# Routed experts of a two-layer mixture kernel: blocks 0 to 3 by sorted rows in place of dense tiles

## The chip, the cores and the metric

One NeuronCore of a Trainium2 chip runs the kernel. The metric is the device time of one execution in microseconds (us), the median of the runs. TensorE is called PE in the rows, its weight loads PEld, VectorE DVE, ScalarE ACT, GpSimd POOL, and SyncE SP; SPq is SP's queue of DMA issues.

## What is computed

The reference adds two layers to x of 32 x 128 tokens with 128 features. Each layer is a conditioning block followed by a feed-forward block. The change is within the conditioning block of the second layer (`_L1_cond_ref`), of which this is the part that matters:

```python
for e in range(N_SHARED):                       # 2 shared experts
    h = silu(x @ s_w1[e].T) * (x @ s_w3[e].T)
    shared_out = shared_out + h @ s_w2[e].T
s = sigmoid(router_in @ W_router.T)             # 8 experts
_, topk_idx = top_k(s + router_bias, 2)
s_sel = take_along_axis(s, topk_idx, axis=1)
gates = where(denom > 1e-09, s_sel / (denom + 1e-09), 1.0 / TOP_K)
for e in range(8):                              # 8 routed experts
    h = gelu(x @ r_w1[e].T)
    routed_out = routed_out + h @ r_w2[e].T * gates_full[:, e:e + 1]
out = (shared_out / 2 + routed_out) / 4
```

A token has a gate other than zero for 2 of the 8 routed experts. The feed-forward block behind it is of low rank: P = x U1, H = gelu(P V1 + b1), y = (H U2) V2 + b2, with rank 32, and the token's x is added.

## The kernel before

The 4096 tokens lie transposed (features on the 128 partitions) in NBLK = 8 blocks of BLK = 512 tokens. fp32 accuracy comes from fp32r matmuls on high and low parts: an up projection of a tile is three of them (high weights by high tokens, low by high, high by low), so is a down projection in the first layer; behind the second layer's hidden tiles the down weights are folded with U1 into WD, four copies of 32 columns, and a down projection is two matmuls, with the high part HH and the low part HL of the hidden tile.

`plan()` writes the work as one list of items. A and G are the conditioning of layer one, B its eight experts (8 experts x 8 blocks x 4 tiles, expert outermost). The second layer's items are S (shared, 4 a block, two up projections each), R (routed, 8 a block, one for each expert over all 512 tokens) and F (feed-forward, 4 a block). The order there is S0 S1 R0 R1, S2 S3 F0 F1 R2 R3, S4 S5 F2 F3 R4 R5, S6 S7 F4 R6 R7, F5 F6 F7, where S0 is all of block 0's S items.

An item has a slot k in the list. TensorE issues its up projection at slot k and its down projection LAG = 5 slots later (`up`, `down`). In between VectorE and ScalarE make the hidden tile Hf (for R: gelu in place, then VectorE multiplies by the gates, line 1558), ScalarE or VectorE its high part HH (lines 1084, 1568) and GpSimd or VectorE its low part HL (lines 1663, 1571), by the item's `hi_act` and `lo_pool`. PSUM has four banks for up projections, two for down sums, two for small uses. The program of each engine is written out in the order of k; engines keep to each other only by semaphores, so SP can run ahead of TensorE.

The routing runs in `choose(g, k)` on VectorE in ten steps for each half g of the blocks (0 to 3 and 4 to 7), at the slots `pick`. The gates are turned by TensorE, copied to q3, written to DRAM (line 730) and from there broadcast to 128 partitions by SP, 256 KB for each block and expert (line 658), into CWB, ST and TMP (`gate_place`). SP's queue also brings the weights of layer one's experts (ST<-in_wb_dram), the combine weights of layer one (CWB<-scratch, line 755), and the weights of layer two (ST<-in_wc_dram, line 737), which VectorE and GpSimd split at the slots `split_wc` (lines 1504, 1611). In G, tokens are brought by DMAs whose address comes from a register: a TENSOR_LOAD on SP brings the register's value (line 761), then the DMA is issued (line 771).

## Time and profile before

| | us |
|---|---|
| median of 3 runs | 889.8 (889.48 to 890.18) |
| span of the profiled execution | 886.9 |
| PE busy | 870.3 (98%) |
| DVE busy | 682.8 (77%) |
| ACT busy | 574.0 (65%) |
| POOL busy | 402.0 (45%) |
| SP's queue q1, share of 16 DMA engines | 30.1% |

The profile is of one execution. Its span runs from the first to the last instruction, and the runs' device time holds what lies around it. A matmul in the rows is shown with its latency, so a busy PE does not mean one at its peak: the distance of two starts is the pace. The layer-two part begins at 703.1 us and is some 184 us long.

### The profile page before, as it was taken

The page shows a single profiled execution, that of the slowest core. Times are in us where ns is not written, and L with a number is a line of the kernel's source. Part 1 is how long each engine was busy: PE and PEld are TensorE (multiplying, and loading weights), DVE is VectorE, ACT ScalarE, POOL GpSimd, SP SyncE. Part 2 cuts the span into 40 slices and gives each one's busy share as a digit, 9 for nine tenths or more (in the row PEclk, how much of TensorE's full clock was granted, in tenths as well). Part 3 has the DMA queues.
Part 4 walks back from the last instruction along what each step waited for, and adds up shares of the span by engine and source line. Part 5 has one row for each costly group of instructions (what it writes and reads, how often), then busy time and mean ns, then how long its engine had stood idle before and what let it go on. Part 6 is the DMA issues. An engine that isn't in the chain of part 4 may idle for free.

```text
span 886.9 us, 12606 instructions
## 1 busy us (share of the span) xinstructions
PE 870.3 (98%) x3838; PEld 690.2 (78%) x3838; DVE 682.8 (77%) x1094; ACT 574.0 (65%) x1029; POOL 402.0 (45%) x376
## 2 busy tenths in 40 slices
PE   8999999999999999999999999999999999999997
PEld 5788888777888888888888888888888777777773
DVE  7877777869689786686686686686665888998887
ACT  7888888765555455555555555555555678989895
POOL 7557783135356453253253252252232227754462
PEclk9999999999999999999999999999999999999999
DMA  9589981023113112012012012011010049582700
GB/s 311 211 276 313 293 295 35 1 86 135 48 48 111 42 42 84 4 45 84 1 48 83 1 48 84 0 48 48 1 48 0 1 108 209 106 178 53 161 25 36
DMA packets 36404, 83.23 MB, mean 94 GB/s; under 512 B 4464, under 2 KB 14320, under 8 KB 34544
## 3 DMA queue, kind: packets, MB, share of 16 engines
q1 hardware_dynamic: 36336, 82.42, 30.1%
q8 instruction: 31, 0.51, 0.2%
q14 instruction: 37, 0.30, 0.1%
HBM read 71.39 MB, written 6.83 MB: 88 GB/s over the span
## 4 chain that ended last, share of the span: by engine, by line
PE 76%; DVE 9%; issue 4%; ACT 3%; SPq 3%; DMA 2%; POOL 1%; DVEq 0%; ACTq 0%; POOLq 0%
PE ps L932 16%; PE ps L951 16%; PE ps L937 16%; PE ps L992 8%; PE ps L994 8%; PE ps L987 8%; DVE HL L1571 3%; SPq L658 1%; PE ps L974 1%; PE ps L972 1%; DVE Hf L1551 1%; DMA ST<-scratch 1%; DVE Hf L1558 1%; ACT HH L1084 1%; SPq L771 1%
## 5 line engine op out<-in xcount | busy, mean ns | idle before, releaser
L1078 ACT ACTIVATE Sg<-ps 128x512 f32<-128x512 f32 x288 | 171.7, 597 | 242.6 <-PE ps L951 242.3
L1551 DVE TENSOR_TENSOR Hf<-ps,Sg 128x512 f32<-128x512 f32 x288 | 197.9, 688 | 147.7 <-ACT Sg L1078 97.5
L1663 POOL TENSOR_TENSOR HL<-Hf,HH 128x512 fp32r<-128x512 f32 x130 | 174.2, 1347 | 157.4 <-ACT HH L1084 141.0
L1084 ACT ACTIVATE HH<-Hf 128x512 fp32r<-128x512 f32 x346 | 216.1, 625 | 21.1 <-DVE Hf L1551 14.4
L1571 DVE TENSOR_TENSOR HL<-Hf,HH 128x512 fp32r<-128x512 f32 x248 | 220.1, 888 | 4.3 <-ACT HH L1084 3.2
L932 PE MATMUL ps<-XHL,WBH 128*128 128x512 f32 x512 | 203.7, 398 | 1.8 <-DVE Hf L1551 1.8
L951 PE MATMUL ps<-XHL,WBH 128*128 128x512 f32 x512 | 202.2, 395 | 0.0
L937 PE MATMUL ps<-XHL,WBL 128*128 128x512 f32 x512 | 202.0, 395 | 0.0
L1678 POOL TENSOR_TENSOR XT<-XT,TMP 128x512 f32<-128x512 f32 x64 | 84.0, 1312 | 248.9 <-DVE TMP L1425 248.7
L932 PEld LDWEIGHTS ps<-XHL,WBH 128*128 128x128 f32 x512 | 96.0, 188 | 27.0 <-DVE Hf L1551 4.0
L951 PEld LDWEIGHTS ps<-XHL,WBH 128*128 128x128 f32 x512 | 96.0, 188 | 23.0
L937 PEld LDWEIGHTS ps<-XHL,WBL 128*128 128x128 f32 x512 | 96.2, 188 | 21.8
L992 PE MATMUL ps<-HH,WBL 128*128 128x512 f32 x256 | 101.0, 395 | 0.0
L987 PE MATMUL ps<-HH,WBH 128*128 128x512 f32 x256 | 100.7, 394 | 0.0
L994 PE MATMUL ps<-HL,WBH 128*128 128x512 f32 x256 | 100.7, 393 | 0.0
L1571 DVE TENSOR_TENSOR HL<-ps,HH 128x512 fp32r<-128x512 f32 (+1 forms) x116 | 69.9, 614 | 30.5 <-ACT HH L1084 29.4
L1071 ACT ACTIVATE ps<-ps,GWU 128x512 f32<-128x512 f32 (+1 forms) x84 | 49.0, 587 | 17.2 <-PE ps L951 17.0
L987 PEld LDWEIGHTS ps<-HH,WBH 128*128 128x128 f32 x256 | 48.0, 187 | 12.0 <-DVE TMP L1425 0.4
L992 PEld LDWEIGHTS ps<-HH,WBL 128*128 128x128 f32 x256 | 48.0, 188 | 11.8
L994 PEld LDWEIGHTS ps<-HL,WBH 128*128 128x128 f32 x256 | 48.1, 188 | 11.2
L932 PE MATMUL ps<-XHL,WCH 128*128 128x512 f32 x128 | 51.2, 400 | 2.0 <-ACT Sg L1078 1.1
L951 PE MATMUL ps<-XHL,WCH 128*128 128x512 f32 x128 | 50.5, 395 | 0.0
(275 smaller groups left out, 1327.6 us busy)
## 6 DMA issues: line engine op xcount, KB each, us to landing
CWB<-scratch SPq DMA_DIRECT2D x14, 1024.0 KB, 4.5
...
```

Source lines behind the costliest of these rows:

```text
L932: e.matmul(o, wh, tokens(it, 0), start=True, stop=False)
L937: e.matmul(o, wl, tokens(it, 0), start=False, stop=False)
L951: e.matmul(o, wh, tokens(it, 1), start=False, stop=True).then_inc(s_z, 1)
L987: e.matmul(bk[:, 0:n], wh, HH[:, hs, 0:n], start=it.new, stop=False)
L992: e.matmul(bk[:, 0:n], wl, HH[:, hs, 0:n], start=False, stop=False)
L994: e.matmul(bk[:, 0:n], wh, HL[:, hs, 0:n], start=False, stop=it.last).then_inc(s_down, 1)
L1078: e.activation(Sg[:, it.n % NG, :], zb[z % NZ][:, :], ACT.Silu).then_inc(s_act, 1)
L1084: e.activation(HH[:, it.n % NH, 0:it.cols], hidden_place(it), ACT.Copy).then_inc(s_hi_act, 1)
L1551: e.tensor_tensor(Hf[:, it.n % NS, :], zb[z % NZ][:, :], Sg[:, it.n % NG, :], ALU.mult).then_inc(s_prod, 1)
L1571: e.tensor_tensor(l, f, h.bitcast(F32), ALU.subtract).then_inc(s_lo_dve, 1)
L1663: e.tensor_tensor(HL[:, it.n % NH, :], Hf[:, it.n % NS, :], HH[:, it.n % NH, :].bitcast(F32), ALU.subtract).then_inc(s_lo_pool, 1)
L1678: e.tensor_tensor(XT[:, it.blk, :], XT[:, it.blk, :], TMP[:, t % 2, :], ALU.add).then_inc(s_acc, 1)
```

## The change

The routed experts of blocks 0 to 3 (ROWS = 2048 tokens) are computed for the two chosen experts of a token only. The tokens' rows are turned by TensorE (`fw`, 4 transposes a block) and copied to XTM. `dispatch` on VectorE gives each of the 4096 pairs of token and expert a position, sorted by expert; POOL writes the rows there with 32 indirect DMAs (`scatter`). The sorted rows are cut into groups of DG = 256 within an expert; the most that there can be is NDG = 23 groups. A table `tiles` says for each group where it lies and which expert it has. SP loads the rows of a group and its expert's weights by registers (`group_place`, `load_xg`, `load_wg`), TensorE turns them, projects up (3 matmuls of 256 columns), and projects down rows by 32 columns (2 fp32 matmuls); SP stores the sums in DRAM. POOL brings each token's two sums back with 32 more indirect DMAs (`gather`), weighs and adds them; TensorE turns them and VectorE adds them to the shared sums PF.

The order becomes S0 to S5, the 23 groups D, R4 R5, S6 S7, F4 F5, R6 R7, F6 F0 F7 F1 F2 F3. The low parts of S tiles, on POOL for blocks 2 and 3 before, are on DVE. F items count as late (with whole fp32 tiles for odd f) from the third block of the order on, six blocks in place of three. The DRAM areas of sorted rows and sums (NZERO = 15 pieces of 786 KB) are filled with zeros from PADS at `zero_fill`, the first slot of layer one's second expert; PADS is cleared by POOL there. The gates of blocks 0 to 3 are no longer broadcast; those of blocks 4 and 5 are, all in one slot behind the second selection, since their `free` is now 0.

The diff, cut to its core:

```diff
-LATE = NBLK - 3
+SPARSE = 4
+ROWS = SPARSE * BLK
+DG = 256
+NDG = 2 * ROWS // DG + 7
+NDT = 8 * ROWS // DG
+NX = 8
+NW = 8
+NXS = 3
+ND = 4
+NRS = 5
+RW = 288
+NZERO = (NDT + 8) * DG * (P + 32) // P // 1536
+FORDER = [4, 5, 6, 0, 7, 1, 2, 3]
+FAT = {b: i for i, b in enumerate(FORDER)}
+LATE = 2
...
-    for b in range(0, NBLK, 2):
-        items += shared(b) + shared(b + 1)
-        for f in (b - 2, b - 1):
-            if 0 <= f < LATE:
-                items += final(f)
-        items += routed(b) + routed(b + 1)
-    for b in range(LATE, NBLK):
+    for b in range(6):
+        items += shared(b)
+    items += [Item("D", g, 0, 0, False) for g in range(NDG)]
+    items += routed(4) + routed(5) + shared(6) + shared(7) + final(4) + final(5)
+    items += routed(6) + routed(7)
+    for b in FORDER[2:]:
         items += final(b)
...
+        load_xg, load_wg = {}, {}
+        for g in range(NDG):
+            load_xg.setdefault(d0 - 3 if g < NX else d0 + g - NX + 1, []).append(g)
+            load_wg.setdefault(d0 - 3 if g < NX else d0 + g - NW + 5, []).append(g)
...
+        fw = {t_b[b] + 3: b for b in range(SPARSE)}
+        fw_copy = {t + 1: b for t, b in fw.items()}
+        p0 = lag_b[3] + 1
+        rank, table = p0 + 8, p0 + 11
+        scatter = {p0 + 10 + t: t for t in range(4 * SPARSE)}
+        gather = {d0 + NDG + 8 + 2 * t: t for t in range(4 * SPARSE)}
+        gathered = {}
+        for b in range(SPARSE):
+            k = d0 + NDG + 8 + 2 * (4 * b + 3) + 2
+            gathered[k if b < 2 else max(k, first_f[b - 2] - 3)] = b
+        zero_fill = pos["B", 0, 1, 0].k
+        pick = [[p0 + i for i in range(15)],
...
+                it.kind == "F" and FAT[it.blk] < LATE and it.k % 2 == 1) or (
+                it.kind == "R" and it.ex % 4 != 1 and (it.blk, it.ex) != (NBLK - 1, 7)) or (
+                it.kind == "S" and it.k < p0 + 10 and it.k % 2 == 1)
...
-        for b in range(NBLK):
+        for b in range(SPARSE, NBLK):
             for ex in range(8):
-                free = pos["R", b - 2, ex, 0].k if b > 1 else done("B", 4 * (ex // 4) + 3, 7, 3)
-                if b == 1:
-                    free = scr_slots["B", 0] + 1
-                gate_slots.setdefault(max(scr_slots["B", b // 4], free) + 1, []).append((b, ex))
+                free = pos["R", b - 2, ex, 0].k if b > SPARSE + 1 else 0
+                gate_slots.setdefault(max(scr_slots["B", 1], free) + 1, []).append((b, ex))
 
...
+                if k == zero_fill + 2:
+                    e.wait_ge(s_clear, 1)
+                    for sorted_d, n in ((xs_d, NZERO * 4 // 5), (rs_d, NZERO // 5)):
+                        flat = sorted_d.rearrange("t r k -> (t r k)").rearrange("(p n) -> p n", p=P)
+                        for i in range(n):
+                            e.dma_start(flat[:, i * 1536:i * 1536 + 1536], ZERO).then_inc(f_zero, 16)
...
+                if k == d0 - 3:
+                    e.wait_ge(f_xs, 16 * 8 * SPARSE)
+                    e.wait_ge(f_rw, 48)
+                    e.wait_ge(s_sorted, 3)
+                    e.wait_ge(s_down, pos["B", NBLK - 1, 7, 3].n + 1)
+                    place = []
+                for g in load_xg.get(k, ()):
+                    place.append(group_place(g))
+                    if g >= NX:
+                        e.wait_ge(s_z, items[d0 + g - NX].z[0] + 1)
+                    src = xs_d[bass.ds(place[g][0], 1)].rearrange("x (c p) k -> p (x c) k", p=P)
+                    e.dma_start(XG[:, g % NX, :, :], src).then_inc(f_xg[g % NX], 16)
+                for g in load_wg.get(k, ()):
+                    if g >= NW:
+                        e.wait_ge(s_dw, g - NW + 1)
+                    src = rw_d[bass.ds(place[g][1], 1)].rearrange("x p k -> (x p) k")
+                    e.dma_start(WG[:, g % NW, :].bitcast(F32), src).then_inc(f_wg[g % NW], 16)
+                if k in group_out:
+                    g = group_out[k]
+                    e.wait_ge(*ab_done.of(("W", g)))
+                    out = rs_d[bass.ds(place[g][0], 1)].rearrange("x (c p) k -> p (x c) k", p=P)
+                    e.dma_start(out, RS[:, g % NRS, :, :]).then_inc(f_rs[g % NRS], 16)
...
+                if k in group_k:
+                    turn_rows(e, items[k])
+                if k in group_u:
+                    group_up(e, group_u[k])
+                if k in group_w:
+                    group_down(e, group_w[k])
+                if k < len(items) and k not in group_k:
...
+        def turn_rows(e, it):
+            g, z = it.blk, it.z[0]
+            e.wait_ge(*z_free(z - NZ))
+            e.wait_ge(f_xg[g % NX], 16 * (g // NX + 1))
+            for c in range(2):
+                mm = e.transpose(group_bank(g)[:, c * P:c * P + P], XG[:, g % NX, c, :], S("ident"))
+            mm.then_inc(s_z, 1)
+
+        def group_up(e, g):
+            o = group_bank(g)[:, DG:2 * DG]
+            w = WG[:, g % NW, :]
+            e.wait_ge(f_wg[g % NW], 16 * (g // NW + 1))
+            e.wait_ge(s_d_lo, g + 1)
+            e.matmul(o, w[:, 0:P], XGHL[:, g % NXS, 0, :], start=True, stop=False)
+            e.matmul(o, w[:, P:2 * P], XGHL[:, g % NXS, 0, :], start=False, stop=False)
+            e.matmul(o, w[:, 0:P], XGHL[:, g % NXS, 1, :], start=False, stop=True).then_inc(s_du, 1)
+
+        def group_down(e, g):
+            bk = ab_bank(("W", g))
+            e.wait_ge(*ab_free(("W", g)))
+            e.wait_ge(s_d_act, g + 1)
+            for c in range(2):
+                mm = e.matmul(bk[:, c * 32:c * 32 + 32], HD[g % ND][:, c * P:c * P + P], WG[:, g % NW, 2 * P:RW].bitcast(F32),
+                              start=True, stop=True)
+            mm.then_inc(s_dw, 1)
...
+                if k in group_k:
+                    g = group_k[k]
+                    e.wait_ge(s_z, items[k].z[0] + 1)
+                    if g >= NXS:
+                        e.wait_ge(s_du, g - NXS + 1)
+                    e.activation(XGHL[:, g % NXS, 0, :], group_bank(g)[:, 0:DG], ACT.Copy).then_inc(s_d_hi, 1)
+                if k in group_u:
+                    g = group_u[k]
+                    e.wait_ge(s_du, g + 1)
+                    if g >= ND:
+                        e.wait_ge(s_dw, g - ND + 1)
+                    e.activation(HD[g % ND], group_bank(g)[:, DG:2 * DG], ACT.Gelu).then_inc(s_d_act, 1)
...
+                        e.indirect_dma_start(xs_d.rearrange("t r k -> (t r) k"),
+                                             bass.IndirectOffsetOnAxis(POS[:, i, t:t + 1], 0), XTM[:, t, :],
+                                             None).then_inc(f_xs, 16)
+                if k in gather:
+                    t = gather[k]
+                    if t == 0:
+                        for g in range(max(0, NDG - NRS), NDG):
+                            e.wait_ge(*stored(g))
+                    for i in range(2):
+                        e.indirect_dma_start(RG[:, t // 4, t % 4, i, :], None, rs_d.rearrange("t r k -> (t r) k"),
+                                             bass.IndirectOffsetOnAxis(POS[:, i, t:t + 1], 0)).then_inc(
+                                                 f_rg[t // 4 % 2], 16)
+                if k in gathered:
+                    b = gathered[k]
+                    e.wait_ge(f_rg[b % 2], 16 * 8 * (b // 2 + 1))
+                    e.wait_ge(s_sorted, 5)
+                    for i in range(2):
+                        r = RG[:, b, :, i, :]
```

On SP, the place where the gates of the first blocks to need them are broadcast, before:

```order
L755 DMA CWB<-scratch 128x2048 [waits s_fin] x3
L730 DMA scratch<-q 128x128 [waits s_ab]
L658 DMA CWB<-scratch 128x512 [waits f_scr10,s_fin] x8
L658 DMA ST<-scratch 128x512 [waits f_scr10,s_w_lo] x6
L658 DMA TMP<-scratch 128x512 [waits f_scr10,s_acc] x2
```

and now (WB holds a group's weights, WB0F its rows, `tiles` the table):

```order
L872 ISA
L872 DMA WB<-routed_weights 128x288
L829 DMA scratch<-q 128x128 [waits s_ab]
L757 DMA CWB<-scratch 128x512 [waits f_scr11,s_fin] x8
L757 DMA ST<-scratch 128x512 [waits f_scr11,s_w_lo] x6
L757 DMA TMP<-scratch 128x512 [waits f_scr11,s_acc] x2
L909 TENSOR_LOAD tiles x2
L867 ISA [waits s_z]
L867 DMA WB0F<-sorted_rows 128x2x128
```

The write and the 16 broadcasts now stand between the loads of group 7 and those of group 8. Further down on SP, the cycle of a group in the D stage, which was not there before:

```order
L872 ISA [waits s_dw]
L872 DMA WB<-routed_weights 128x288
L877 ISA [waits s_ab]
L877 DMA sorted_sums<-RS 128x2x32
L909 TENSOR_LOAD tiles x2
L867 ISA [waits s_z]
L867 DMA WB0F<-sorted_rows 128x2x128
```

A weight load, the store of the group eight before, two register loads and a row load follow each other in one queue. On POOL, the low parts of the routed tiles, before:

```order
L1678 TENSOR_TENSOR XT<-XT,TMP 128x512 [waits s_acc,s_fin] x2
L1663 TENSOR_TENSOR HL<-Hf,HH 128x512 [waits s_hi_act] x2
L1663 TENSOR_TENSOR HL<-Hf,HH 128x512 [waits s_hi_dve]
L1663 TENSOR_TENSOR HL<-Hf,HH 128x512 [waits s_hi_act] x2
L1663 TENSOR_TENSOR HL<-Hf,HH 128x512 [waits s_hi_dve]
```

and now, at R4 and R5, where WB0F takes the gathered sums:

```order
L2047 TENSOR_TENSOR HL<-Hf,HH 128x512 [waits s_hi_act] x2
L2047 TENSOR_TENSOR HL<-Hf,HH 128x512 [waits s_hi_dve]
L2047 TENSOR_TENSOR HL<-Hf,HH 128x512 [waits s_hi_act] x2
L1978 DMA WB0F<-sorted_sums,POS 128x32 [waits f_rs1,f_rs0,f_rs2,f_rs4,f_rs3]
L1978 DMA WB0F<-sorted_sums,POS 128x32
L2047 TENSOR_TENSOR HL<-Hf,HH 128x512 [waits s_hi_dve]
L2047 TENSOR_TENSOR HL<-Hf,HH 128x512 [waits s_hi_act]
L1978 DMA WB0F<-sorted_sums,POS 128x32 x2
L2047 TENSOR_TENSOR HL<-Hf,HH 128x512 [waits s_hi_act]
L1978 DMA WB0F<-sorted_sums,POS 128x32 x2
L2047 TENSOR_TENSOR HL<-Hf,HH 128x512 [waits s_hi_dve]
L2047 TENSOR_TENSOR HL<-Hf,HH 128x512 [waits s_hi_act]
```

The 32 gathers moved in between the HL tiles, two at a time. On SP in layer one, around the first slots of the second expert, before:

```order
L668 DMA CWB<-scratch 128x512 x3
L726 DMA ST<-in_wb_dram 128x1536 [waits s_w_lo]
L755 DMA CWB<-scratch 128x2048 [waits s_fin]
L737 DMA ST<-in_wc_dram 128x1024 [waits s_w_lo] x2
L755 DMA CWB<-scratch 128x2048 [waits s_fin]
```

and now:

```order
L767 DMA CWB<-scratch 128x512 x3
L825 DMA ST<-in_wb_dram 128x1536 [waits s_w_lo]
L846 DMA sorted_rows<-XGHLF 128x1536 [waits s_clear]
L846 DMA sorted_rows<-XGHLF 128x1536 x11
L846 DMA sorted_sums<-XGHLF 128x1536 x3
L891 DMA CWB<-scratch 128x2048 [waits s_fin]
L836 DMA ST<-in_wc_dram 128x1024 [waits s_w_lo] x2
L891 DMA CWB<-scratch 128x2048 [waits s_fin]
```

The zero fill stands ahead of a load of combine weights and the two loads of layer-two weights.

## Rows read from the trace of the kernel before

**Rows 1.** The page: busy time by engine, and GB/s in 40 slices.
```profile
PE 870.3 (98%) x3838; PEld 690.2 (78%) x3838; DVE 682.8 (77%) x1094; ACT 574.0 (65%) x1029; POOL 402.0 (45%) x376
...
GB/s 311 211 276 313 293 295 35 1 86 135 48 48 111 42 42 84 4 45 84 1 48 83 1 48 84 0 48 48 1 48 0 1 108 209 106 178 53 161 25 36
```

**Rows 2.** TensorE in time order, 62 to 63 us: start, duration, instruction.
```profile
62.72 0.40 PE L994 MATMUL ps<-HL,GWD 128*128 128x512 f32 x1
62.96 0.28 PE L932 MATMUL ps<-GHL,GWU 128*128 128x256 f32 x1
63.08 0.28 PE L937 MATMUL ps<-GHL,GWU 128*128 128x256 f32 x1
```

**Rows 3.** Busy time in stretches of layer two: engines, clock, DMA share, GB/s.
```profile
703.10:800.90 97.80, 93.71 (x399) 72.69 (x399) 85.57 (x150) 78.82 (x135) 51.98 (x39) 1.00 0.62 136
723.40:742.40 19.00, 19.00 (x86) 15.44 (x85) 15.39 (x25) 15.71 (x29) 12.08 (x10) 1.00 0.87 192
758.60:765.60 7.00, 6.18 (x26) 4.33 (x25) 5.71 (x11) 6.75 (x12) 4.97 (x4) 1.00 0.48 103
765.60:785.20 19.60, 19.60 (x83) 14.91 (x83) 19.01 (x28) 18.17 (x33) 15.09 (x12) 1.00 0.60 133
807.90:827.60 19.70, 19.18 (x83) 15.27 (x82) 19.41 (x29) 17.99 (x33) 14.96 (x12) 1.00 0.62 140
827.60:842.70 15.10, 15.10 (x65) 11.91 (x65) 12.55 (x20) 11.80 (x20) 4.14 (x4) 1.00 0.66 131
842.70:845.50 2.80, 2.80 (x13) 2.25 (x12) 1.18 (x3) 2.77 (x5) 0.00 (x0) 1.00 0.36 99
865.00:886.90 21.90, 15.87 (x50) 8.39 (x48) 15.69 (x24) 12.61 (x21) 4.48 (x4) 0.99 0.10 37
```

**Rows 4.** SP's queue in time order, 62 to 66 us: dynamic DMAs.
```profile
62.24 0.33 SPq L775 DMA_DIRECT2D GWU<-expert_up  x1
63.38 2.45 SPq L771 DMA_DIRECT2D GX<-XT  x4
```

**Rows 5.** Line 761, register loads: nanoseconds min/median/max, first and last start.
```profile
L761 SPq TENSOR_LOAD <-index x42: 268/298/952, 33.6 to 124.0; - x42
L761 POOLq TENSOR_LOAD <-index x21: 322/792/1339, 44.2 to 144.7; - x21
```

**Rows 6.** Line 771, the 64 KB DMAs: us from issue to landing, min/median/max.
```profile
DMA to landing us min/median/max: 1.8/3.0/5.5
```

**Rows 7.** SP's queue in time order, 716 to 736 us: the 16 gate broadcasts.
```profile
715.84 0.32 SPq L730 DMA_DIRECT2D scratch<-q  x1
...
732.56 3.98 SPq L658 DMA_DIRECT2D TMP<-scratch  x2
```

**Rows 8.** VectorE in time order, 710 to 712 us.
```profile
710.48 0.28 DVE L1389 TENSOR_TENSOR q<-q,r 128x128 f32<-128x128 f32 x1
...
711.12 0.38 DVE L1394 TENSOR_TENSOR q<-q 128x128 f32<-128x128 f32 x1
...
711.93 0.68 DVE L1571 TENSOR_TENSOR HL<-Hf,HH 128x512 fp32r<-128x512 f32 x1
```

**Rows 9.** SP's queue in time order, 238 to 256 us.
```profile
238.83 0.32 SPq L755 DMA_DIRECT2D CWB<-scratch  x1
255.19 0.81 SPq L737 DMA_DIRECT2D ST<-in_wc_dram  x2
```

**Rows 10.** VectorE in time order, at 266.8 us: the first split of layer-two weights.
```profile
266.81 1.41 DVE L1504 CAST WCH<-ST 128x512 fp32r<-128x512 f32 x1
```

**Rows 11.** VectorE's groups from 865 us on: count, busy us, mean ns, idle before.
```profile
L1571 DVE TENSOR_TENSOR HL<-Hf,HH 128x512 fp32r<-128x512 f32 x7 | 5.4, 768 | 0.3
L1568 DVE CAST HH<-Hf 128x512 fp32r<-128x512 f32 x7 | 4.0, 567 | 0.6 <-ACT Hf L1071 0.6
L1536 DVE SCALAR_TENSOR_TENSOR QS<-PH,sm,ps 128x512 fp32r<-128x512 f32 x3 | 2.2, 748 | 1.7 <-ACT PH L1049 1.7
```

**Rows 12.** GpSimd in time order, at 679.2 us: its 128x512 instruction.
```profile
679.20 1.30 POOL L1678 TENSOR_TENSOR XT<-XT,TMP 128x512 f32<-128x512 f32 x1 [4.42 <-DVE TMP L1425]
```

365 lines of the change are left out of this document (310 added, 55 removed).

## The prediction

> **What bounds the kernel now.** I read the first two parts of the page first [rows 1]: TensorE has a matmul in flight for 98% of the span, so time is won only by giving TensorE less to do and lost wherever it is made to wait. A matmul of 512 columns starts 0.23 us after the one before, one of 256 columns 0.12 us [rows 2]; the 0.40 of a single one is its latency. Then I cut the second layer into its blocks [rows 3]: the dense routed experts take 19.0 us for blocks 0 and 1 and 19.6 for blocks 2 and 3, 38.6 together, at a granted clock of 1.00. VectorE is busy for 15.4 and 19.0 us of it, near to a second bound, but TensorE is the one that never rests. Last I read the queues that the change loads: SyncE's DMA queue [rows 4 to 7] and GpSimd [rows 5, 12]. Neither matters today, because SP has only the gate broadcasts to issue and they run ahead of their use.
>
> **What is taken away.** 32 dense R tiles of 5 matmuls: 32 x 5 x 0.232 = 37.1 us by spacing, 38.6 us by the windows. I take **-38.6**.
>
> **The groups on TensorE.** A group is 2 transposes, 3 matmuls of 256 columns (3 x 0.12 = 0.36 us) and 2 small fp32 matmuls. I take 0.1 us of spacing for each of the four small ones, a little under the 0.12 of 256 columns: 0.76 us a group, 23 x 0.8 = 18 us. If TensorE set the pace the change would win 20 us here. It does not, I think, and the reason is SP.
>
> **The queue of SP in the D stage.** All loads and stores of the groups are issued by SP in program order, behind registers that are loaded one by one. Prices: four DMAs with a computed address take 2.45 us, 0.61 each; one with longer rows 0.33; the two register loads of a group fit in the 0.8 us between 62.24 + 0.33 and 63.38 [rows 4], with 0.27 to 0.95 us for a single load [rows 5]. So a row load is 0.8 + 0.6 = 1.4, a store 0.6, and a weight load 0.43: 0.33 and the 0.1 us of address work. The order behind the scatters is: 8 row loads and 8 weight loads, 8 x 1.4 + 8 x 0.43 = 14.6 us; then the write of the gates of blocks 4 to 7 and all 16 broadcasts of blocks 4 and 5. Today such a write and its 16 broadcasts take the queue from 715.84 to 732.56 + 3.98 = 736.5, 20.7 us [rows 7], at a DMA share of 0.87 and 192 GB/s [rows 3], so they are bound by the transfers and will not be faster. Only then the loads of groups 8 to 12 (5 x 1.4 = 7.0), the ten groups that load, weigh and store (10 x 2.43 = 24.3) and the five that only weigh and store (5.2): 36.5 us. The last weights land 3.0 us after their issue [rows 6]. The first 8 groups, all that is prefetched, are done by TensorE within the 20 us of broadcasts, and it then waits. From the landing of the last scatter the stage lasts 14.6 + 20.7 + 36.5 + 3 = **74.8 us**. The bounds: 0.27 instead of 0.8 us for register loads that find their value ready takes 12 us off, 0.95 + 0.27 adds 10.
>
> **When the scatters land.** The positions are ready about where today's last selection step is, 711 us [rows 8], plus 9 us that the changes ahead cost (below) plus 3 for the longer chain with its trip over TensorE: 723. Then POOL issues 32 indirect DMAs. The trace has none. From below stands SP's issue of a DMA, 0.33 us [rows 4]; from above the 3.0 us until a DMA of 64 KB lands [rows 6], if each had to be through before the next. POOL's own rows are 0.79 us for a register load and 1.30 us for an instruction over 128 partitions [rows 5, 12], and POOL has to make 128 addresses; I take their middle, **1.05 us**: 33.6 us, the last landing at 723 + 33.6 + 3 = 759.6. The Trainium skill ("DMA: Bandwidth & Descriptors", Latency and other measured facts) states about 1 us to the first byte for a DMA issued from GpSimd; by it the sum would be 2 us lower here. No row here shows one.
>
> The D stage thus ends at 759.6 + 74.8 = 834.4.
>
> **The shared tiles before it.** S0 to S5 now stand in a row, and the low parts of S2 and S3 move from GpSimd to VectorE, where the others are. Today they take 97.8 - 38.6 - 7.0 = 52.2 us (the stretch of S0 to S5 without R0 to R3 and F0, F1) [rows 3]. VectorE then has 24 x 2 x 0.68 = 32.6 us for the tiles, some 65 small steps of the routing at 0.26 us = 17 (those of 128 columns take 0.28, the smaller ones less), and 7 whole steps beside the tiles at 0.68 = 5 [rows 8]: 55 us, **+3** (0 to 6). So TensorE is at the first group at 703.1 + 9 + 55 = 767.1, and the D stage costs 834.4 - 767.1 = **+67.3**, against the 38.6 taken away.
>
> **Zero fill in the B stage.** 15 DMAs of 786 KB, 11.8 MB, enter SP's queue at about 229 us (the second expert's first slot, 19 slots of 2.09 us before 266.8, and the memset), ahead of the combine weights issued at 238.8 and of the weights of layer two (255.2), which VectorE needs at 266.8 [rows 9, 10]. At 295 GB/s, a usual slice of the busy start [rows 1], they take 40 us, and the 2 MB behind them 7: 276, 9 us late. Some 3 us are covered by the tiles in flight: **+6**. At the 313 GB/s of the fastest slice it is 4, at the 192 of the broadcasts 30; nothing below zero, since no work is taken away there.
>
> **TensorE outside the D stage.** 16 transposes of the rows, 3 matmuls for the ranks with their wait on VectorE: 16 x 0.1 + 1.4 = **+3** (1 to 5). Both +6 and +3 are in the 9 above.
>
> **The gathers.** POOL issues 32 more, two every second slot, in the same program order as the HL tiles that TensorE waits for. Stretch by stretch, 8 gathers each (8.4 us): block R5 has 6 HL x 1.30 [rows 12] = 7.8 and a mixing step of about 1.9 (640 columns in all, by the 1.30 for 512), 18.1 against 9.8 us of TensorE, half of the 19.7 of two such blocks [rows 3]; the LAG of 5 slots covers 4.5: stall 4. The shared tiles after it (15.1 us) need no HL from POOL and catch up. F4 and F5: 8.4 + 5.2 against 2 x 3.15 (between the 2.8 of F4 and 3.5 of F0) with 3.5 covered: 4. R6: 3.5 carried + 8.4 + 7.8 against 9.8: 5. Sum **+13**; 0 at 0.33 us a gather, about 43 at 2 us.
>
> **Final tiles.** Six blocks instead of three now come at the end with nothing between them. There VectorE is the bound: 2 x (0.57 + 0.77) + 3 x 0.75 + 0.69 for the mix = 5.6 us a block [rows 11]. Today F0 to F4 take 7.0 + 7.0 (F2 and F3, like F0 and F1) + 2.8 = 16.8 and the last three with their tail 21.9, 38.7 in all [rows 3]. After: F4 and F5 6.3, the six 33.6, the tail 6.3: 46.2, **+7.5** (3 to 10).
>
> **Sum.** -38.6 + 6 + 3 + 3 + 67.3 + 13 + 7.5 = +61.2. 886.9 + 61.2 = 948.1 of span; the median of the runs is 889.8, 2.9 above the span: **951 us**, 6.9% slower.
>
> **Rivals.** (A) The loads are hidden after all and the groups run at TensorE's pace: 18 us in place of 38.6. For it: eight groups are prefetched, and today's queue of SP never holds anyone (its broadcasts begin behind 715.8 and the last of them is used some 30 us later). Then -38.6 + 18 + 3 + 3 and no more than 5 for the rest: 877 span, 880 us, faster. It decides if SP's whole work from the 9th group on, 20.7 + 36.5 us, falls under some 25 us; only if a computed address, a register load and a full queue cost under half of what the queue shows [rows 4, 5, 7]. The Trainium skill ("DMA: Bandwidth & Descriptors", Issuing engines are not separate DMA queues) speaks for this one: it calls the time to start a DMA usually small beside the DMA itself. The trace agrees for one DMA (0.61 against 3.0 us), but here 69 of them and 46 register loads stand in one queue. Chance 0.08. (B) Indirect DMAs are as cheap as SP's, 0.33 us: the scatters land at 736, the broadcasts wait for the gates until about 766 (the second selection, at the end of S5), D ends at 766 + 20.7 + 36.5 + 3 = 826, 8 us sooner, and no gather stalls anyone, 13 us: 930 us. Still slower, and so is everything under 0.8 us, where the gates are the later ones. Chance 0.15. (C) They cost 2 us or more: scatters land at 790, D ends at 865, gathers stall 43: from 61.2 up by 30 + 30, 1011 us, and with a slow zero fill 1035. Chance 0.14. (D) The gains and losses meet within 0.2%: 0.02. My forecast, with SP and POOL as bounds and a price of 0.7 to 1.6 us, has 0.61.
>
> **How the numbers follow.** The forecast's own range, 915 to 985, comes from the bounds of register loads (-12, +10), of the zero fill (-3, +24), of the final tiles (-4, +3) and of a price of 0.7 to 1.6 (-17, +27), of which not all fall together. To leave out no more than 0.2, the range takes in (B) with short register loads and an early zero fill, and the near part of (C): 905 to 1005. A measurement of this kernel tells about 0.2% from no change: faster 0.08, same 0.02, slower 0.90.
>
> **What would show it.** The new profile should have (1) TensorE waiting at the first group's transposes or up matmuls for a DMA, until about 15 us after the last scatter; (2) a wait of over 15 us at the 9th group while SP issues 16 broadcasts; (3) groups 13 to 22 coming every 2.4 us, not every 0.8; (4) on TensorE waits for HL of POOL in R5, F4 and R6; (5) one wait of VectorE on a DMA near 267 us; (6) six final blocks at 5 to 6 us each. The prediction is wrong if groups follow each other at 0.8 to 1 us, or if SP gets ahead of TensorE in the D stage; and its size is wrong above all with the price of an indirect DMA, which moves it by 32 us (and the stalls) for each us.

## Result and the profile after

The changed kernel takes 987.6 us (median of 4 runs, 987.12 to 987.93) against 890.0 (889.48 to 890.32): 1.110 times as long, 95% interval 1.1083 to 1.1114. It lies in the range of the prediction, 905 to 1005, but 37 us above the 951 that was named. The profiled execution has a span of 985.0 us, so what lies around the span is again 2 to 3 us. One later execution of the kernel before, beside the combined kernel at the end of the experiments, took 1057.9 us at a granted clock of 0.75; it is in no ratio.

The page of the kernel after, against [rows 1]: busy time by engine, and the clock in 40 slices.

```profile
PE 897.4 (91%) x3922; PEld 715.3 (73%) x3922; DVE 674.1 (68%) x1130; ACT 557.3 (57%) x1016; POOL 422.7 (43%) x417
...
PEclk9999999999999999999999999999986865798989
```

TensorE is no longer busy all the time, and from the 31st slice on its clock is below full speed in most slices. The stretches of layer two after, against [rows 3]: start and end, length, busy us (instructions) of PE, PEld, DVE, ACT and POOL, granted clock, DMA share, GB/s.

```profile
704.95:785.20 80.25, 59.16 (x217) 44.21 (x216) 47.77 (x116) 34.55 (x59) 36.21 (x36) 0.81 0.18 55
785.20:806.40 21.20, 8.28 (x61) 7.13 (x59) 5.27 (x14) 6.90 (x17) 0.00 (x0) 0.79 0.66 159
806.40:845.70 39.30, 30.35 (x142) 28.51 (x143) 8.64 (x31) 11.91 (x31) 0.00 (x0) 0.50 0.59 145
845.70:931.30 85.60, 70.20 (x256) 52.07 (x256) 52.98 (x78) 51.49 (x89) 66.69 (x66) 0.88 0.33 67
931.30:985.00 53.70, 32.57 (x105) 19.45 (x104) 32.56 (x52) 24.69 (x41) 8.27 (x9) 0.94 0.08 29
```

They are S0 to S5 with the routing; the D stage up to the ninth group and the rest of it; R4 to R7 with S6, S7, F4 and F5; the six final blocks. Set against the sum of the prediction:

| stretch | predicted | measured | difference |
|---|---|---|---|
| start of layer two | 709.1 (703.1 + 6) | 704.95 | -4.1 |
| S0 to S5, with transposes and ranks | 58.0 | 80.3 | +22.3 |
| D stage | 67.3 | 60.5 | -6.8 |
| R4 to R7 with S6, S7, F4, F5 | 73.7 | 85.6 | +11.9 |
| six final blocks and the tail | 39.9 | 53.7 | +13.8 |
| span | 948.1 | 985.0 | +37 |

The fourth row of the prediction is 19.7 + 4, 15.1, 6.3 + 4 and 19.6 + 5; the fifth 33.6 + 6.3.

**SP's queue in the D stage went as foretold.** The queue in time order, 757 to 817 us:

```profile
760.01 8.86 SPq L867 DMA_DIRECT2D WB0F<-sorted_rows  x8
769.06 4.37 SPq L872 DMA_DIRECT2D WB<-routed_weights  x8
784.75 0.33 SPq L829 DMA_DIRECT2D scratch<-q  x1
786.34 6.95 SPq L757 DMA_DIRECT2D CWB<-scratch  x8
...
806.35 5.92 SPq L867 DMA_DIRECT2D WB0F<-sorted_rows  x5
...
814.24 0.38 SPq L867 DMA_DIRECT2D WB0F<-sorted_rows  x1
...
816.55 0.38 SPq L867 DMA_DIRECT2D WB0F<-sorted_rows  x1
```

The preload of eight groups takes 13.4 us (predicted 14.6). The write of the gates and the 16 broadcasts take 21.6 us, from 784.75 to the next row load (predicted 20.7, from [rows 7]), and then a group passes every 2.3 us, 814.24 to 816.55 (predicted 2.43). The longest of TensorE's waits between 785 and 846 us (us in total, times, longest):

```profile
PE ps L1081 <- DMA WB0F<-sorted_rows: 20.6, 1, 20.6
```

One wait of 20.6 us at the ninth group, from 793.8 to 814.3. The last 8 us of it pass after the row load's issue at 806.35 (a landing took 2.1 us in the median and 7.8 at most): it lands behind the broadcasts, with the DMA engines 0.73 to 0.89 busy. What was not foretold is the gap in SP's queue before it, from 773.4 to 784.75: the gates of blocks 4 to 7 were not there yet. And behind the wait it is TensorE, not SP, that sets the pace of most groups. Transposes of the ninth, tenth, 18th and 19th group:

```profile
814.33 0.66 PE L1081 MATMUL ps<-sm,WB0F 128*128 128x128 f32 x2 [20.57 <-DMA WB0F<-sorted_rows]
816.13 0.67 PE L1081 MATMUL ps<-sm,WB0F 128*128 128x128 f32 x2
...
831.19 0.67 PE L1081 MATMUL ps<-sm,WB0F 128*128 128x128 f32 x2
833.55 0.67 PE L1081 MATMUL ps<-sm,WB0F 128*128 128x128 f32 x2
```

From the ninth group to the 16th one starts every 1.81 us at a granted clock of 0.50, with no idle time; only the 18th to the 21st come 2.2 to 2.9 us apart, at SP's pace, and the last two 1.8 to 1.9. In all of 806 to 846 us TensorE waits 0.9 us for weights and, after 814.3, for no rows.

**What was not foreseen lies in S0 to S5.** From 740 us on TensorE, ScalarE and VectorE stand still together. ScalarE and VectorE after, and the matmuls that end the tiles they wait for (in brackets the idle time before an instruction, and its releaser; "remote" is a releaser that the profile cannot name):

```profile
737.66 0.39 PE L1155 MATMUL ps<-XHL,WCH 128*128 128x512 f32 x1
738.36 0.39 PE L1155 MATMUL ps<-XHL,WCH 128*128 128x512 f32 x1
739.52 0.39 PE L1155 MATMUL ps<-XHL,WCH 128*128 128x512 f32 x1
747.44 0.60 ACT L1307 ACTIVATE Sg<-ps 128x512 f32<-128x512 f32 x1 [8.76 <-remote]
752.40 0.69 DVE L1895 TENSOR_TENSOR Hf<-ps,Sg 128x512 f32<-128x512 f32 x1 [10.98 <-issue]
761.45 0.60 ACT L1307 ACTIVATE Sg<-ps 128x512 f32<-128x512 f32 x1 [12.89 <-remote]
```

Sg is made from the first up projection of a tile, Hf from Sg and the second. So the Sg at 747.44 needs the matmul of 737.66, the Hf at 752.40 that of 738.36, and the Sg at 761.45 that of 739.52. By the trace this last one was over at 739.91; ScalarE, idle since 748.6, began 21.5 us after its end. The trace also holds the times at which TensorE's semaphore rose for these three: 747.42, 752.33 and 761.43, each less than 0.1 us before the engine that waited for it started. So ScalarE and VectorE act at once, and it is TensorE's semaphore that is late. (The ends of matmuls in a trace are modelled; but TensorE had started five more behind the one of 739.52 by 742 us.) In between GpSimd does one thing (ns min/median/max of one, first and last start):

```profile
L1969 POOL DMA_INDIRECT sorted_rows<-WB0F,POS x32: 954/962/1303, 715.5 to 756.7; - x32
```

32 scatters, 0.96 us each and 0.30 to the next: one every 1.26 us. They were priced at 1.05, and the last was expected to land at 759.6; SP begins its row loads at 760.01.

### The profile page after: what moved, and what is told of

The parts are those of the page before. It is cut to its first block, busy times and chain, and to the rows that moved or that the text cites. A ratio compares the mean times of both kernels' runs of the same rounds, so it can differ in the third digit from the quotient of the medians.

```text
span 985.0 us, 13148 instructions
## 1 busy us (share of the span) xinstructions
PE 897.4 (91%) x3922; PEld 715.3 (73%) x3922; DVE 674.1 (68%) x1130; ACT 557.3 (57%) x1016; POOL 422.7 (43%) x417
## 3 DMA queue, kind: packets, MB, share of 16 engines
q0 software_dynamic: 2048, 2.63, 1.0%
## 4 chain that ended last, share of the span: by engine, by line
PE 72%; POOL 6%; DVE 5%; issue 5%; SPq 4%; ACT 3%; another core or an unknown queue 2%; DMA 2%; ACTq 0%; DVEq 0%; POOLq 0%
PE ps L1136 15%; PE ps L1141 14%; PE ps L1155 14%; PE ps L1191 8%; PE ps L1196 8%; PE ps L1198 8%; POOL HL L2047 3%; POOL WB0F L1978 2%; SPq L757 2%; PE ps L1171 1%; DVE HL L1915 1%; DVE Hf L1895 1%; SPq L909 1%; SPq L867 1%
## 5 line engine op out<-in xcount | busy, mean ns | idle before, releaser
L1313 ACT ACTIVATE HH<-Hf 128x512 fp32r<-128x512 f32 x316 | 197.2, 624 | 30.4 <-DVE Hf L1895 15.9
L1136 PE MATMUL ps<-XHL,WB 128*128 128x512 f32 x512 | 203.0, 396 | 2.8 <-DVE Hf L1895 2.8
L2047 POOL TENSOR_TENSOR HL<-Hf,HH 128x512 fp32r<-128x512 f32 x92 | 122.3, 1334 | 189.9 <-ACT HH L1313 187.2
L1141 PE MATMUL ps<-XHL,WB 128*128 128x512 f32 x512 | 201.8, 394 | 0.0
L1155 PE MATMUL ps<-XHL,WB 128*128 128x512 f32 x512 | 200.3, 391 | 0.0
L1136 PEld LDWEIGHTS ps<-XHL,WB 128*128 128x128 f32 x512 | 96.1, 188 | 28.1 <-DVE Hf L1895 5.5
L1155 PEld LDWEIGHTS ps<-XHL,WB 128*128 128x128 f32 x512 | 96.1, 188 | 21.9
L1141 PEld LDWEIGHTS ps<-XHL,WB 128*128 128x128 f32 x512 | 96.2, 188 | 20.2
L1196 PE MATMUL ps<-HH,WB 128*128 128x512 f32 x256 | 100.9, 394 | 0.0
L1191 PE MATMUL ps<-HH,WB 128*128 128x512 f32 x256 | 100.6, 393 | 0.0
L1198 PE MATMUL ps<-HL,WB 128*128 128x512 f32 x256 | 100.2, 391 | 0.0
L1136 PE MATMUL ps<-XHL,WCH 128*128 128x512 f32 x96 | 44.2, 461 | 19.6 <-ACT Sg L1307 7.2
L1191 PEld LDWEIGHTS ps<-HH,WB 128*128 128x128 f32 x256 | 48.1, 188 | 11.8 <-DVE TMP L1754 0.4
L1198 PEld LDWEIGHTS ps<-HL,WB 128*128 128x128 f32 x256 | 48.1, 188 | 11.0
L1196 PEld LDWEIGHTS ps<-HH,WB 128*128 128x128 f32 x256 | 48.1, 188 | 10.6
L1313 ACT ACTIVATE HH<-ps 128x512 fp32r<-128x512 f32 (+1 forms) x89 | 48.1, 541 | 0.0
```

The lines of the kernel that those rows point to most:

```text
L1136: e.matmul(o, wh, tokens(it, 0), start=True, stop=False)
L1141: e.matmul(o, wl, tokens(it, 0), start=False, stop=False)
L1155: e.matmul(o, wh, tokens(it, 1), start=False, stop=True).then_inc(s_z, 1)
L1191: e.matmul(bk[:, 0:n], wh, HH[:, hs, 0:n], start=it.new, stop=False)
L1196: e.matmul(bk[:, 0:n], wl, HH[:, hs, 0:n], start=False, stop=False)
L1198: e.matmul(bk[:, 0:n], wh, HL[:, hs, 0:n], start=False, stop=it.last).then_inc(s_down, 1)
```

## Experiments

All are single edits of the changed kernel unless said otherwise. A time is of one execution beside the kernel before (889.1 to 890.9), except where an interval is given. Layer two began between 702.5 and 705.6 us in these runs, with the same code ahead of it, so a total carries about 2 us that have nothing to do with the edit; the stretches don't.

### The scatters left out

```diff
-                        e.indirect_dma_start(xs_d.rearrange("t r k -> (t r) k"),
-                                             bass.IndirectOffsetOnAxis(POS[:, i, t:t + 1], 0), XTM[:, t, :],
-                                             None).then_inc(f_xs, 16)
...
-                    e.wait_ge(f_xs, 16 * 8 * SPARSE)
+                    e.wait_ge(f_zero, 16 * NZERO)
```

> The changed kernel without its 32 scatters (the rows of blocks 0 to 3 are not written, so the groups compute on the zeros of the fill). In the changed kernel S0 to S5 last 79.4 us instead of the 58 that I had summed up, with TensorE, ScalarE and VectorE all idle between 740 and 761 us while GpSimd issues indirect DMAs without a break. Theory 1: it is the scatters that hold up the signals of finished matmuls. Then S0 to S5 fall to 55 to 60 us (20 less), the second selection is ready at about 765, the 16 gate broadcasts go out then, and the D stage ends at about 826 in place of 845.7: some 966 us. Theory 2: it is the routing itself, its steps on VectorE that stand between the tiles, or TensorE's lower clock. Then S0 to S5 keep 75 us or more, and the time stays at 980 to 987.

958.8 us, 28.8 less. Its stretch S0 to S5:

```profile
702.80:758.00 55.20, 51.55 (x218) 38.62 (x217) 47.05 (x116) 33.80 (x59) 4.56 (x4) 1.00 0.14 41
```

Theory 1. S0 to S5 take 55.2 us with the routing in them, at the full clock, so neither the routing nor VectorE cost more than was summed up. The second selection was ready at 757.7, 8 us sooner than I had put it, and D ended at 817.2 instead of 826.

### The gate broadcasts between the group loads

```diff
-                gate_slots.setdefault(max(scr_slots["B", 1], free) + 1, []).append((b, ex))
+                when = max(scr_slots["B", 1], free) + 1
+                if b < SPARSE + 2:
+                    when = d0 + 5 + 8 * (b - SPARSE) + ex
+                gate_slots.setdefault(when, []).append((b, ex))
```

> The changed kernel with one order changed: the 16 gate broadcasts of blocks 4 and 5 stand one by one between the loads and stores of groups 12 to 27 instead of all ahead of group 8. Theory 1 (SP issues in order and the block of 16 holds up everything behind it for 20.6 us, while the loads of groups leave the DMA engines mostly free): SP is held until the gates are written (784.75), then 5.9 us of row loads, 10 cycles of 2.29 + 0.5 and the rest, 42 to 45 us; D ends at about 830 in place of 845.7: 970 us. Theory 2 (the transfers are the bound, wherever they stand, or TensorE's chain within a group is): D ends within 5 us of 845.7, 982 to 988 us.

973.7 us, 13.9 less; D takes 47.8 us in place of 60.5 and ends at 831.0. SP's queue in one cycle of it:

```profile
803.87 0.38 SPq L870 DMA_DIRECT2D WB0F<-sorted_rows  x1
...
805.47 0.41 SPq L760 DMA_DIRECT2D CWB<-scratch  x1
806.66 0.38 SPq L870 DMA_DIRECT2D WB0F<-sorted_rows  x1
```

A broadcast adds 0.5 us to a cycle of now 2.8, so 16 of them cost 8 us of SP's time where the block of 16 had cost 21.6. That was theory 1: the same bytes in another order of one queue, and the wait at the ninth group is gone. Here SP does set the pace: TensorE waits for weights 12 times, 9.8 us in all, and a group takes 2.5 to 3.1 us.

### Plain loads in place of the gathers

```diff
-                    for i in range(2):
-                        e.indirect_dma_start(RG[:, t // 4, t % 4, i, :], None, rs_d.rearrange("t r k -> (t r) k"),
-                                             bass.IndirectOffsetOnAxis(POS[:, i, t:t + 1], 0)).then_inc(
-                                                 f_rg[t // 4 % 2], 16)
...
+                if k in gather and gather[k] % 4 == 0:
...
+                        e.dma_start(RG[:, b, 2 * h:2 * h + 2, :, :].rearrange("p t i k -> p (t i) k"), src).then_inc(
+                            f_rg[b % 2], 16)
```

> The changed kernel with the 32 gathers on GpSimd replaced by 8 plain loads of the same bytes from SP's queue (the sums arrive unsorted; the weighing and adding stays on GpSimd). Theory 1: GpSimd's 1.26 us for each gather is what makes R5, S6, S7 and R6, R7 long: from R4's first up projection to the end of R7 there are 85.6 us, against the 60.6 that these blocks take at TensorE's pace before. Then this stretch loses 18 to 25 us: 962 to 970. My prediction had 13 us for the gathers: 975. Theory 2: the stretch is long for another reason, the order of the blocks or the lower granted clock, and less than 8 us go: 980.

962.4 us, 25.2 less. R4 to R7 with S6, S7, F4 and F5, first this kernel's stretch, then TensorE's waits for low parts in the changed kernel (here they are one of 1.2 us):

```profile
842.90:905.60 62.70, 60.83 (x256) 46.78 (x256) 52.48 (x78) 50.70 (x89) 37.72 (x34) 0.98 0.46 91
```

```profile
PE ps L1178 <- POOL HL L2047: 14.7, 11, 2.9
```

GpSimd is busy for 37.7 us instead of 66.7, its waits are gone, and the stretch falls by 22.9 us. Up to 14.7 us of that are TensorE's own waits for low parts; the clock is also higher, 0.98 in place of 0.88, and no run splits the rest between it and waits of the engines in between. Theory 1; the 13 us of the prediction were 10 too few.

### Whole tiles only in the last three final blocks

```diff
-LATE = 2
+LATE = 5
```

> The changed kernel with LATE = 5 in place of 2: of the six final blocks at the end only the last three use whole fp32 tiles for odd f, as before the change; the order of the work stays. Theory 1: the whole tiles (1.02 us of TensorE at a time, with a trip to ScalarE between) make the chain of a final block 8.2 us long, against the 4 to 5 of the last three blocks before. Then three blocks lose 2 to 3 us each: 978 to 981 us. Theory 2: the chain over the sums of the routed part (mixed sums, PH, PS, QS) sets the 8.2 us, and the time stays within 2 us of 987.6.

982.2 us, 5.3 less, but only 3.5 of it in the final blocks:

```profile
930.20:980.40 50.20, 30.23 (x105) 19.81 (x104) 36.28 (x52) 28.03 (x47) 16.90 (x15) 0.90 0.08 32
```

Between the theories. Whole tiles explain 3.5 of the 13.8 us that the final blocks took above the sum. The other part is by the trace a chain; no run takes it away. The waits of TensorE in the final blocks of the changed kernel, and VectorE's rows of the sums that end a block there:

```profile
PE ps L1111 <- DVE PS L1857: 7.4, 3, 3.7
PE ps L1176 <- DVE QS L1864: 6.7, 3, 2.2
```

```profile
964.42 0.75 DVE L1864 SCALAR_TENSOR_TENSOR QS<-PH,sm,ps 128x512 fp32r<-128x512 f32 x1 [1.71 <-ACT PH L1266]
972.49 0.75 DVE L1864 SCALAR_TENSOR_TENSOR QS<-PH,sm,ps 128x512 fp32r<-128x512 f32 x1 [1.64 <-ACT PH L1266]
```

These two blocks end 8.1 us apart. Over all six the sums are made at 949.39, 955.83, 964.42, 972.49, 977.97 and 980.22, 6.2 us apart on average. VectorE is idle before each: it waits for ScalarE's PH, which waits for TensorE, which waits for VectorE's PS or QS of the block before.

### Half of the scatters

```diff
-                    for i in range(2):
+                    for i in range(1):
```

> The changed kernel with 16 scatters in place of 32: only the first chosen expert of each token gets its row, the other half of the rows stays zero. In the changed kernel TensorE's first late signal comes about 22 us after the first scatter, when 17 or 18 of them have been issued. Theory 1 (something fills up with the number of indirect DMAs issued in a row, and signals are late only once it is full): 16 scatters in 20 us hold up nothing, S0 to S5 last 55 to 57 us, and the time is near that without scatters, 959 to 962 us. Theory 2 (each indirect DMA costs TensorE its share, at whatever number): S0 to S5 last about half way between 55 and 80 us, some 67, and the time is about 973.

968.5 us. S0 to S5:

```profile
704.80:766.60 61.80, 54.32 (x218) 39.71 (x217) 46.81 (x116) 33.84 (x59) 20.53 (x20) 0.94 0.18 54
```

61.8 us, 6.6 above the kernel without scatters; 32 of them cost 25. Neither theory: fewer than 17 are enough to hold signals up, and the cost is not in proportion either. By these two kernels it grows as the stream goes on.

### Limits on the scatters that are under way

Three kernels. In the first GpSimd waits for each scatter before it issues the next:

```diff
                     for i in range(2):
+                        if 2 * t + i:
+                            e.wait_ge(f_xs, 16 * (2 * t + i))
```

> The changed kernel with all 32 scatters, but GpSimd issues each one only when the one before has landed. Theory 1 (the late signals come from indirect DMAs issued without a break, 1.26 us apart): with the breaks S0 to S5 fall to 55 to 62 us; but the scatters then take some 32 x 2.5 = 80 us, land at about 795, and SP's preloads, broadcasts and loads (13 + 21 + 37 us) start from there: D ends at about 870, the time is 1005 to 1015. Theory 2 (the kind or the number of the DMAs does it, not the missing break): S0 to S5 keep 75 us or more, or grow with the scatters, and the time is over 1010.

1027.3 us. Its scatters, and S0 to S5:

```profile
L1971 POOL DMA_INDIRECT sorted_rows<-WB0F,POS x32: 957/957/1485, 716.1 to 807.3; - x32
...
DMA to landing us min/median/max: 2.2/2.2/4.2
```

```profile
705.60:766.10 60.50, 52.94 (x217) 39.76 (x215) 46.43 (x116) 33.62 (x59) 21.91 (x20) 0.94 0.05 18
```

The signals are on time (60.5 us, most of the 5.3 above 55.2 is a wait for XT, whose last sum stands behind the slower scatters in GpSimd's program). The scatters take 2.94 us each, and the stages behind them are late by as much. A scatter of 64 KB lands 2.2 us after its issue. The Trainium skill ("DMA: Bandwidth & Descriptors", Anatomy of one DMA — SWDGE (gpsimd) path) gives 2.0 us and the bytes by 436 KB/us for a DMA issued from GpSimd, 2.15 us here; the trace agrees. It says nothing of a stream of them beside other engines.

In the next two, each slot of a small ring of semaphores must be free before its next scatter, with two or four slots:

```diff
+                        n = 2 * t + i
+                        if n >= 2:
+                            e.wait_ge(f_xw[n % 2], 16 * (n // 2))
...
-                                             None).then_inc(f_xs, 16)
+                                             None).then_inc(f_xw[n % 2], 16)
```

> The changed kernel with all 32 scatters, where GpSimd issues one only when the one two before has landed: at most two are under way. With one at a time TensorE's signals were on time, but a scatter took 2.8 us; without any limit they came every 1.26 us and the signals were late. Theory 1 (a backlog of indirect DMAs delays the signals): the pace becomes 1.4 to 1.6 us, S0 to S5 last 55 to 65 us, the scatters land at about 765, and the stages behind them (13 + 21 + 39 us) end at about 838: 977 to 981 us. Theory 2 (the rate of issue does it, however many are under way): the pace stays near 1.26 us, the signals stay late, S0 to S5 last 72 to 80 us, 984 to 988 us.

983.7 us. The scatters, and S0 to S5:

```profile
L1974 POOL DMA_INDIRECT sorted_rows<-WB0F,POS x32: 954/958/1364, 713.0 to 764.4; - x32
```

```profile
702.50:758.80 56.30, 51.30 (x217) 38.59 (x215) 48.15 (x116) 33.69 (x59) 32.85 (x32) 1.00 0.10 32
```

1.66 us a scatter, and not one signal is late: 56.3 us. The total hardly moves, since the scatters now land 8 us later and SP's whole queue, preload, broadcasts and groups, starts from there; TensorE now waits 10.7 us for the rows of the first group, and from there D lasts 71.5 us.

> The same with at most four scatters under way. Theory 1 (a backlog of indirect DMAs delays the signals, and it is longer than four): the pace stays 1.26 us for most of them, late signals become few, S0 to S5 last 55 to 65 us; the scatters land at 757, the second selection is ready at about 765, D ends at 830: 970 us. Theory 2 (never more than four are under way in the changed kernel either, so that the limit changes nothing, and the rate does it): S0 to S5 last 78 to 81 us, 985 to 988 us.

985.5 us. Theory 2: scatters from 715.2 to 756.5 us, as without a limit, and S0 to S5 80.2 us. A scatter lands in 2.2 to 4.2 us and one is issued every 1.26, so there are two or three under way in any case.

### Groups at fixed places

```diff
-                    place.append(group_place(g))
+                    place.append((g, g % 8))
...
-                    src = xs_d[bass.ds(place[g][0], 1)].rearrange("x (c p) k -> p (x c) k", p=P)
+                    src = xs_d[place[g][0]:place[g][0] + 1].rearrange("x (c p) k -> p (x c) k", p=P)
```

> The changed kernel without its register loads in the D stage: SP loads and stores the groups at fixed places (group g at rows 256 g, expert g mod 8) in place of those of the table. Theory 1 (SP's issue sets the pace of a group, 2.29 us, and the two register loads with the computed addresses are over a third of it): the cycle falls to about 1.5 us, the 22 us behind the last broadcast go down by 12 to 15, D ends at 831 to 834 in place of 845.7, and the time is 973 to 976 us. Theory 2 (the cycle is set by the chain of a group through TensorE, ScalarE, VectorE and the landing of its store and loads): the cycle stays over 2 us, and under 4 us go.

987.3 us, nothing won. SP's queue in a cycle, and in time order where only stores are left; then the part of D behind the broadcasts:

```profile
816.09 0.47 SPq L872 DMA_DIRECT2D WB<-routed_weights  x1
...
817.59 0.47 SPq L872 DMA_DIRECT2D WB<-routed_weights  x1
...
828.63 0.36 SPq L877 DMA_DIRECT2D sorted_sums<-RS  x1
...
830.44 0.36 SPq L877 DMA_DIRECT2D sorted_sums<-RS  x1
```

```profile
803.40:841.10 37.70, 28.67 (x142) 28.70 (x143) 8.57 (x31) 11.87 (x31) 0.00 (x0) 0.50 0.65 153
```

The cycle falls from 2.3 to 1.5 us as theory 1 said, but the stretch only from 39.3 to 37.7: SP has its loads out ahead, and from there a group is stored every 1.81 us (828.63 to 830.44). That is the pace at which TensorE, at a clock of 0.50 since the wait for the broadcasts, starts all 15 groups here, and the pace of the ninth to the 16th in the changed kernel as well. In the first groups, at the full clock, a group takes 0.98 us in the changed kernel. So the outcome is that of theory 2, by the mechanism of neither: two bounds lie close together, and the register loads, over a third of SP's cycle, cost the changed kernel no more than 1.6 us there.

> The changed kernel with the gate broadcasts between the group loads, and with groups at fixed places (no register loads). With fixed places alone only 0.3 us went although SP's cycle fell from 2.29 to 1.5 us, and the last groups then followed each other every 1.81 us. Theory 1 (a group's own trip over TensorE at the lower clock, ScalarE and VectorE costs 1.8 us, and that is the next bound right below SP's): SP's cycle falls from 2.80 to about 2.0, the stage from 47.8 to 36 to 40 us, and the time from 973.7 to 962 to 966 us. Theory 2 (register loads never mattered, the transfers and landings set the pace): the stage stays over 45 us, 971 us or more.

949.4 us, 13 us below the best that theory 1 allowed. But its S0 to S5 took 56.9 us, 23.3 less than with the broadcasts between the loads alone, nearly the whole gain:

```profile
702.50:759.40 56.90, 51.81 (x217) 38.52 (x216) 48.77 (x117) 34.00 (x59) 36.85 (x36) 1.00 0.13 42
...
780.00:806.80 26.80, 21.85 (x104) 20.27 (x105) 6.20 (x22) 8.45 (x22) 0.00 (x0) 0.51 1.02 237
```

and its scatters were issued as fast as ever:

```profile
L1972 POOL DMA_INDIRECT sorted_rows<-WB0F,POS x32: 954/958/1295, 713.0 to 754.9; - x32
```

GpSimd's program is the same as with the broadcasts between the loads alone, where the scatters ran from 713.5 to 754.5 and S0 to S5 took 80.2 us. The two kernels differ only in how SP addresses the groups' loads and stores, and these come after S0 to S5. So 32 scatters without a pause can also pass without a late signal. (The two ran on different chips, 8 and 14 in the record; but the kernel with at most four under way was late on chip 14 too.) This run takes away the simple reading, that the rate alone decides. For the D stage it says little: it begins here while the rows are still being loaded and lasts 47.4 us, against 47.8; from 780 on the DMA engines are full (share 1.02, 237 GB/s), which may be the bound behind SP and TensorE.

### Together

> The changed kernel with three of the edits together: at most two scatters under way, the 16 gate broadcasts between the group loads, and whole fp32 tiles for the last three final blocks only. If the three mechanisms are separate: signals on time; scatters landed at 765 as in the run with two under way, preload until 781, then no wait for the gates (the second selection is ready at about 760) and groups at SP's cycle of 2.80 us: R4 begins at 828 to 831, R4 to R7 as before, the final blocks 5 us shorter: 963 to 968 us, 8.3 to 8.8% slower than the kernel before. If the gain of the broadcasts depended on the wait for the second selection, it is lost here, and the time is 976 to 980.

967.05 us (median of 4, 965.7 to 968.1), 1.087 times the kernel before (1.0839 to 1.0896). It is what the separate mechanisms gave, and 20.5 us less than the changed kernel with the same result: the best that was found of this order of work, and still 77 us slower than the dense tiles.

> The changed kernel with all four costs taken away at once: no scatters (rows stay zero), plain loads from SP in place of the gathers (sums arrive unsorted), gate broadcasts between the group loads, whole tiles in the last three final blocks only. One by one they took off 28.8, 25.2, 13.9 and 5.3 us, 73.2 together. If they are separate: 987.6 - 73.2 = 914 us, 910 to 920, still 2 to 3% slower than the kernel before, which would show that the order of blocks and the groups themselves cost more than the dense tiles. If they overlap by more than 10 us (the gates' wait and the scatters' are both before group 8): 924 to 935. Below 890 only if they amplify each other.

923.6 us. Its D stage and its final blocks:

```profile
758.00:804.60 46.60, 37.15 (x204) 32.06 (x202) 14.63 (x45) 18.69 (x48) 0.00 (x0) 0.66 0.71 184
...
869.80:921.70 51.90, 33.93 (x105) 22.36 (x104) 36.33 (x51) 28.10 (x47) 16.03 (x15) 0.81 0.08 30
```

The four costs sum to 73.2 us one by one and to 64.0 together; in part they overlap. With all of them gone the kernel is 34 us slower than before: the D stage alone, 46.6 us, is longer than the 38.6 of the dense tiles that it replaces, and the final blocks take 51.9. In this D stage TensorE waits 9.1 us for weights, and SP still loads its registers.

## Why the prediction was right, and where its sum was not

- **Sign, and the wait at the ninth group: right.** A queue of SP that the loads, the register loads and the broadcasts share in program order makes TensorE wait; preload 13.4 (14.6), broadcasts 21.6 (20.7), cycle 2.3 (2.43), the wait at the ninth group 20.6 us. The run with the broadcasts between the loads shows that the order is the cause. Rival (A), loads that are hidden, did not happen. The Trainium skill's sentence that spoke for it ("DMA: Bandwidth & Descriptors", Issuing engines are not separate DMA queues), that starting a DMA is usually cheap beside the DMA, holds for one of them here as well (0.37 us for a row load against a landing of 2.1) and misled for the queue as a whole, in which the block of broadcasts stood before the next rows.
- **Behind the broadcasts: the number right, the bound only in part.** The sum had 36.5 + 3 = 39.5 us of SP's work there, and 39.3 passed. But the prediction had no term for the clock, and put a group on TensorE at 0.8 us. It takes 0.98 at a clock of 1.00 and 1.81 at the 0.50 that TensorE had from 797.4 to 852.1 us. From the ninth to the 16th group TensorE sets the pace and SP is ahead of it, which the prediction had named as a sign of being wrong. The run with fixed places shows it: SP's cycle falls to 1.5 us and only 1.6 us go, where the prediction gave 12 for shorter register loads. That two bounds lay so close is luck.
- **The price of an indirect DMA: nearly right.** 1.26 us, not 1.05; the positions came 8 us sooner (715.5 instead of 723), and the two errors cancel in the landing of the last, which is luck too.
- **"The shared tiles before it", +3: its term was right and the stretch wrong.** 55.2 us without scatters, as summed up; with them 80.3. That the scatters could slow down engines that do not wait for them was no rival of mine. It cost 25.1 us in S0 to S5. It moved the D stage by the part that SP's queue could not hide: the gates came at 784.75 in place of 774.2 (my 759.6 and 14.6), so D ended at 845.7 instead of 834.4. And D began later than predicted, so that its own length is shorter than the 67.3 of the sum.
- **"The gathers", +13: mis-sized, 22.9 measured.** The stalls were summed block by block with a credit for the LAG of five slots and for catching up in S6 and S7; but GpSimd's program runs on into S6 and S7 with 8 gathers and a mixing step, and the low parts of R5 stand in front of TensorE there, 22.7 us for S6 and S7 in place of the 15.1 of [rows 3]. That is 7.6 of the 11.9 us that the stretch has too much; R6 and R7 (29.2 instead of 24.6) have the rest. The stretch of S6 and S7 after, in which TensorE's longest wait, at 883.61 us, is 2.94 us for a low part from GpSimd:

```profile
869.60:892.30 22.70, 18.22 (x66) 13.94 (x65) 13.05 (x19) 11.05 (x18) 19.42 (x21) 0.85 0.34 60
```

- **"Final tiles", +7.5: the wrong bound.** VectorE's work per block was right (32.56 us in six blocks, 5.4 each, 5.6 predicted), but it is not what bounds: it is idle for 21 of 53.7 us. By the trace the blocks stand in a chain of three engines, with up to 8.6 us from one sum to the next; only the part of the whole tiles, 3.5 us, is shown by a run. A busy share near one would have been the test for "VectorE is the bound"; the last three blocks before the change ended 2.4 to 2.8 us apart (876.19, 879.03, 881.42 in VectorE's rows of QS), and only the changed kernel has blocks with a second sum to add.
- **"Zero fill", +6: too much.** SP's queue and VectorE's split of the weights after, against [rows 9, 10]:

```profile
230.07 14.63 SPq L846 DMA_DIRECT2D sorted_rows<-XGHLF  x12
...
257.82 1.54 SPq L836 DMA_DIRECT2D ST<-in_wc_dram  x2
```

```profile
269.51 1.41 DVE L1833 CAST WCH<-ST 128x512 fp32r<-128x512 f32 x1
```

The split has no idle time before it: VectorE did not wait for the weights. What is left is 1.9 us at the start of layer two, no more than the scatter of the other runs (702.5 to 705.6, against 703.1 before).
- **What would show it:** (2) and (4) came so. (3) came in part: groups 13 to 22 start 2.1 us apart on average, between 1.8 and 2.9, not 2.4. (1), (5) and (6) did not: the first group was ready and waiting for TensorE (with two scatters under way, where the signals are on time, TensorE does wait there, 10.7 us), the weights were in time, and the final blocks took 53.7 us with the tail where 39.9 were summed.

The total was inside the range because the range had been kept wide for the price of an indirect DMA; it was not this price that used it up. The largest part of the miss, 25.1 us in S0 to S5, came from something that the sum had at nothing.

**Open:** what makes TensorE's signals late. It is not chance from one execution to the next of the changed kernel, whose four have spans of 984.4 to 985.6 us; most of the others were run once. They were late in seven kernels that issue scatters without waiting for them or with up to four under way, the changed one among them (with half of the scatters to a lesser degree), never in the five that issue none or wait so that at most two are under way, and not in one whose GpSimd program is the same as in one of the seven. In no kernel were they late without scatters in close succession; these alone are not enough. Which state of which queue decides it no run here separates.
